# Weight transposes moved to ScalarE's queue, the second normalised copy replaced by a broadcast row, and the evacuations moved behind the state product

## The reference

```python
xn = (x - mean) / sqrt(var + 1e-5)
# recurrent branch
x2 = xn * rsqrt(mean(xn*xn) + 1e-6) * norm_w
f = maximum(sigmoid(x2 @ w_forget.T), 0.9);  v = x2 @ w_input.T;  o = sigmoid(x2 @ w_output.T)
h = f[..., None]*h + (1-f)[..., None]*v[..., None, :];  y = o * h.sum(-1)   # per head
s = xn + y
# feed-forward branch
e = argmax(xn @ W_router);  inter = gelu(xn @ W1[e] + b1[e])
g = silu(layer_norm(inter @ Wo + bo + xn))
out = x + s * g
```

## Time and profile before

| | us |
|---|---|
| median of two runs | 3336.88 |
| the profiled execution | 3346.98 |
| span of its slowest core, core 0 | 3345.2 |
| spans of all cores | 3309.5 to 3345.2 |
| TensorE busy over the span | 2899.7 (87%) |
| VectorE busy | 705.6 (21%) |
| ScalarE busy | 470.0 (14%) |

### The profile page before, as it was taken

How to read it: one execution, slowest core, us unless ns; L and a number is a source line. 1 busy time by engine, 2 the same in 40 slices (tenths; PEclk the granted TensorE clock), 3 DMA queues, 4 the chain that set the end, 5 groups by cost and what they waited for, 6 DMA issues and landing times.

```text
span 3345.2 us, 32665 instructions; the slowest of 8 cores (3309.5 to 3345.2 us)
## 1 busy us (share of the span) xinstructions
PE 2899.7 (87%) x13376; PEld 1266.5 (38%) x13376; DVE 705.6 (21%) x1289; ACT 470.0 (14%) x733; POOL 245.2 (7%) x349
## 2 busy tenths in 40 slices
PE   0247787877999999999999999999999999999994
PEld 0113333333443444443444444444444444444342
DVE  0326665751003100210111012002200310121003
ACT  1122223210000111020112011101110011102001
POOL 1014353400000000000000000000000000000000
PEclk9768998888999999999999999999999999999997
DMA  9999999945343454435344533433454345434531
GB/s 132 105 124 118 129 155 126 104 86 181 139 154 135 139 176 151 138 140 176 139 151 139 182 145 145 175 146 139 151 176 152 138 139 178 175 113 142 172 126 63
DMA packets 262385, 476.14 MB, mean 142 GB/s; under 512 B 204700, under 2 KB 204700, under 8 KB 216988
## 3 DMA queue, kind: packets, MB, share of 16 engines
q1 hardware_dynamic: 79424, 341.87, 31.4%
q0 software_dynamic: 182816, 132.18, 24.7%
HBM read 482.44 MB, written 81.79 MB: 169 GB/s over the span
## 4 chain that ended last, share of the span: by engine, by line
PE 70%; DMA 4%; DVE 1%; issue 1%; ACT 1%; DVEq 0%; SPq 0%; ACTq 0%; POOL 0%; POOLq 0%
PE pre L622 53%; PE y2a L643 7%; PE y2b L643 6%; DMA w1sl<-w1s 4%; PE pre L629 2%; DVE y L679 0%; DVE y L675 0%; PE pmu L656 0%; DMA wosl<-wos 0%; PE y2b L648 0%; PE y2a L648 0%; PE pmu L572 0%; PE psq L661 0%; DVEq L96 0%; ACT g_bf L761 0%
## 5 line engine op out<-in xcount | busy, mean ns | idle before, releaser
L622 PE MATMUL pre<-maskedA,w1sl 128*128 128x512 bf16 x8192 | 1836.0, 383 | 53.3 <-DMA w1sl<-w1s 53.3
L622 PEld LDWEIGHTS pre<-maskedA,w1sl 128*128 128x128 bf16 x8192 | 786.9, 99 | 1036.6 <-issue 143.6
L785 ACT ACTIVATE interA<-pre 128x512 bf16<-128x512 f32 x256 | 152.9, 597 | 1768.0 <-PE pre L629 1767.8
L643 PE MATMUL y2a<-interA,wosl 128*128 128x512 bf16 x1024 | 241.4, 397 | 2.3 <-DMA wosl<-wos 1.3
L643 PE MATMUL y2b<-interA,wosl 128*128 128x512 bf16 x1024 | 226.2, 379 | 0.0
L718 DVE COPY mask_bf<-pmb 4x512 bf16<-4x512 bf16 x8 | 3.3, 412 | 987.9 <-PE pmb L589 987.9
L162 POOL DMA_DIRECT2D w1s<-w x256 | 187.7, 755 | 296.4 <-issue 296.4
L456 PE MATMUL pj<-xn_fm,wfT 128*128 128x512 bf16 x512 | 121.9, 398 | 77.1 <-ACT f_fm L243 48.8
L417 PE MATMUL trA<-ident_bf,xn_tm 128*128 128x128 bf16 x256 | 34.0, 275 | 140.6 <-DVEq L96 103.6
L643 PEld LDWEIGHTS y2a<-interA,wosl 128*128 128x128 bf16 x1024 | 103.1, 101 | 138.3 <-issue 28.6
L456 PE MATMUL pj<-xn_fm,wiT 128*128 128x512 bf16 x512 | 121.2, 398 | 33.6 <-DVE v_bf L325 19.5
(11 more groups left out here) (115 smaller groups left out, 1244.6 us busy)
## 6 DMA issues: line engine op xcount, KB each, us to landing
w1sl<-w1s SPq DMA_DIRECT2D x256, 1024.0 KB, 5.3
wosl<-wos POOLq DMA_DIRECT2D x64, 1024.0 KB, 5.7
w1s<-w POOLq DMA_DIRECT2D x256, 128.0 KB, 22.3
x_a<-x SPq DMA_DIRECT2D x8, 2048.0 KB, 17.7
x_b<-x SPq DMA_DIRECT2D x8, 2048.0 KB, 17.3
out<-y POOLq DMA_DIRECT2D x8, 2048.0 KB, 8.4
wos<-wo POOLq DMA_DIRECT2D x8, 1024.0 KB, 49.5
xnbf_s<-xn_fm SPq DMA_DIRECT2D x8, 1024.0 KB, 22.8
```

The source lines that it names most:

```text
L622: ins = te.matmul(pre[b][:, :], w1sl[gi % 2][:, off:off + 128], maskedA[:, (e * KC + k) * TT:(e * KC + k + 1) * TT], start=first, stop=False)
L643: ins = te.matmul(y2[b][:, :], wosl[wi_ % 2][:, ic * 128:(ic + 1) * 128], interA[:, ic * TT:(ic + 1) * TT], start=(ic == 0), stop=False)
L785: ti(sc.activation(interA[:, i_abs * TT:(i_abs + 1) * TT], pre[b][:, :], AF.Gelu), "pre_F%d" % b, 1)
```

## The change

- **Weights.** The three casts go out in the order forget, input, output on one semaphore (`s_wnat`). The 24 transposing DMAs are issued by ScalarE (`wt_transposes`), in turn 0, behind `accums(1)` and `sqrtf(1)`, once all three casts are done. TensorE waits once, for all 24, ahead of the first projection of tile 0.
- **Second copy.** `xn2_tm`, its 4 VectorE operations and its 32 transposes per tile are gone. VectorE computes the ratio of the two roots per token (`stt[:, 72:76]`), TensorE transposes it into a row with four 128x1 transposes, ScalarE copies the row to `rrow_bf`, TensorE spreads it over 128 partitions with one matmul into `trB[1]`, and VectorE makes `xn2_fm` from `xn_fm`, the norm's weight and `trB[1]` in 8 `scalar_tensor_tensor` operations.
- **Order on VectorE.** There is no `trevacs`. The evacuations of tile t+1 stand at the head of turn t+1, so behind lines 397 and 401 of turn t. The expert choice stands ahead of the clamp instead of behind the scan.
- Some semaphores and a list of PSUM tiles that nothing used are gone.

```diff
@@ gpsimd
-                    ti(g.dma_start(out=wnat_s[1 * D:2 * D, :], in_=wiw[:, :]), "s_wn0", 16)
-                    ti(g.dma_start(out=wnat_s[0 * D:1 * D, :], in_=wf[:, :]), "s_wn1", 16)
-                    ti(g.dma_start(out=wnat_s[2 * D:3 * D, :], in_=wow[:, :]), "s_wn2", 16)
+                    for widx, src in enumerate([wf, wiw, wow]):
+                        ti(g.dma_start(out=wnat_s[widx * D:(widx + 1) * D, :], in_=src[:, :]),
+                           "s_wnat", 16)
@@ sync
-                    W(sy, "s_wn0", 16)
-                    for k in range(KC):
-                        ti(sy.dma_start_transpose(
-                            wiT[:, k * D:(k + 1) * D],
-                            wnat_s[1 * D:2 * D, k * 128:(k + 1) * 128]), "s_wt", 16)
...
@@ scalar
+                    def wt_transposes():
+                        W(sc, "s_wnat", 48)
+                        for widx in range(3):
+                            for k in range(KC):
+                                ti(sc.dma_start_transpose(
+                                    wTs[widx][:, k * D:(k + 1) * D],
+                                    wnat_s[widx * D:(widx + 1) * D, k * 128:(k + 1) * 128]),
+                                   "s_wt", 16)
...
                     for t in range(NT):
+                        W(sc, "trB_R0", t + 1)
+                        ti(sc.copy(rrow_bf[0:1, :], trB[0][0:1, 0:TT]), "s_rrow", 1)
                         if t + 1 < NT:
                             sqrtf(t + 1)
+                        if t == 0:
+                            wt_transposes()
@@ vector, xnts
-                        for sub in range(SUB):
-                            v.tensor_scalar(xn2_tm[:, sub * D:(sub + 1) * D],
-                                            x_buf[t % 2][:, sub * D:(sub + 1) * D],
-                                            stt[:, 8 + sub:9 + sub], stt[:, 44 + sub:45 + sub],
-                                            OP.subtract, OP.mult)
+                        v.reciprocal(stt[:, 68:72], stt[:, 40:44])
+                        v.drain()
+                        v.tensor_tensor(stt[:, 72:76], stt[:, 44:48], stt[:, 68:72], OP.mult)
                         DR(v, "sv_xn", "s_xfree")
@@ vector, head of turn t (trevacs is gone)
+                        for k in range(KC):
+                            g_ = 8 * t + k
+                            p_ = g_ % 2
+                            W(v, "trA_R%d" % p_, g_ // 2 + 1)
+                            ti(v.tensor_copy(xn_fm[t % 2][:, k * TT:(k + 1) * TT],
+                                             trA[p_][:, :]), "trA_F%d" % p_, 1)
+                        DR(v, "ss_xnev")
+                        W(v, "trB_R1", t + 1)
+                        for k in range(KC):
+                            v.scalar_tensor_tensor(xn2_fm[:, k * TT:(k + 1) * TT],
+                                                   xn_fm[t % 2][:, k * TT:(k + 1) * TT],
+                                                   norw_cm[:, k:k + 1], trB[1][:, :],
+                                                   OP.mult, OP.mult)
+                        DR(v, "sv_x2ev", "trB_F1")
@@ tensor
                         W(te, "sv_lgF", t)
+                        W(te, "s_rrow", t)
+                        for sub in range(SUB):
+                            ins = te.transpose(trB[0][0:1, sub * 128:(sub + 1) * 128],
+                                               stt[:, 72 + sub:73 + sub], ident_f[:, :])
+                        ti(ins, "trB_R0", 1)
...
-                            W(te, "trB_F%d" % p_, g_ // 2)
-                            for sub in range(SUB):
-                                ins = te.transpose(
-                                    trB[p_][:, sub * 128:(sub + 1) * 128],
-                                    xn2_tm[:, sub * D + k * 128: sub * D + (k + 1) * 128],
-                                    ident_bf[:, :])
-                            ti(ins, "trB_R%d" % p_, 1)
+                        W(te, "trB_F1", t)
+                        W(te, "s_rrow", t + 1)
+                        ti(te.matmul(trB[1][:, :], ones_bf[0:1, :], rrow_bf[0:1, :],
+                                     start=True, stop=True), "trB_R1", 1)
...
                         W(te, "sv_x2ev", t + 1)
+                        if t == 0:
+                            W(te, "s_wt", 16 * 24)
                         for pi, wT in enumerate([wiT, wfT, woT]):
-                            if t == 0:
-                                if pi == 0:
-                                    W(te, "s_wt", 16 * 8)
...
```

More of the change, by code:

```diff
@@ L123, in build_core @@
                    EA(nc.psum_tensor("trA1", [128, TT], BF16))]
[L124 to L125 removed]
+            trB = [EA(nc.psum_tensor("trB0", [128, TT], F32)),
+                   EA(nc.psum_tensor("trB1", [128, TT], F32))]
+            rrow_bf = EA(nc.sbuf_tensor("rrow_bf", [1, TT], BF16))
             pj = [EA(nc.psum_tensor("pj0", [128, TT], F32)),
@@ L328, in _ @@
                             xnts(t + 1)
[L329 to L332, removed]
-                            v.tensor_scalar(f_fm[:, c * TT:(c + 1) * TT],
-                                            f_fm[:, c * TT:(c + 1) * TT], FORGET_LB, None,
-                                            OP.max)
-                        v.drain()
-                        for h in range(KC):
-                            b = h % 2
-                            W(v, "vb_R%d" % b, 4 * t + h // 2 + 1)
-                            ti(v.scalar_tensor_tensor(negu_bf[:, h * TT:(h + 1) * TT],
-                                                      f_fm[:, h * TT:(h + 1) * TT], 1.0,
-                                                      vbp[b][:, :], OP.subtract, OP.mult),
-                               "vb_F%d" % b, 1)
-                        v.drain()
-                        if t % 4 != 0:
-                            nS3 = negS_bf[:, :].rearrange("p (h tt) -> p h tt", h=KC)
-                            v.tensor_copy(carry[:, :].rearrange("p (h o) -> p h o", o=1),
-                                          nS3[:, :, TT - 1:TT])
-                            v.drain()
-                        for h in range(KC):
-                            init = 0.0 if t % 4 == 0 else carry[:, h:h + 1]
-                            v.tensor_tensor_scan(negS_bf[:, h * TT:(h + 1) * TT],
-                                                 f_fm[:, h * TT:(h + 1) * TT],
-                                                 negu_bf[:, h * TT:(h + 1) * TT],
-                                                 init, OP.mult, OP.add)
-                        if t + 2 < NT:
-                            vstats(t + 2)
                         W(v, "s_lgR", t + 1)
@@ L392, in _ @@
                         v.drain()
-                        if t + 1 < NT:
-                            trevacs(t + 1)
+                        for c in range(KC):
+                            r = 24 * t + 8 + c
+                            b = r % 2
+                            W(v, "pj_F%d" % b, r // 2 + 1)
+                            v.tensor_scalar(f_fm[:, c * TT:(c + 1) * TT],
+                                            f_fm[:, c * TT:(c + 1) * TT], FORGET_LB, None,
+                                            OP.max)
+                        v.drain()
+                        for h in range(KC):
+                            b = h % 2
+                            W(v, "vb_R%d" % b, 4 * t + h // 2 + 1)
+                            ti(v.scalar_tensor_tensor(negu_bf[:, h * TT:(h + 1) * TT],
+                                                      f_fm[:, h * TT:(h + 1) * TT], 1.0,
+                                                      vbp[b][:, :], OP.subtract, OP.mult),
+                               "vb_F%d" % b, 1)
+                        v.drain()
+                        if t % 4 != 0:
+                            nS3 = negS_bf[:, :].rearrange("p (h tt) -> p h tt", h=KC)
+                            v.tensor_copy(carry[:, :].rearrange("p (h o) -> p h o", o=1),
+                                          nS3[:, :, TT - 1:TT])
+                            v.drain()
+                        for h in range(KC):
+                            init = 0.0 if t % 4 == 0 else carry[:, h:h + 1]
+                            v.tensor_tensor_scan(negS_bf[:, h * TT:(h + 1) * TT],
+                                                 f_fm[:, h * TT:(h + 1) * TT],
+                                                 negu_bf[:, h * TT:(h + 1) * TT],
+                                                 init, OP.mult, OP.add)
+                        if t + 2 < NT:
+                            vstats(t + 2)
                         W(v, "ss_o", t + 1)
```

35 lines of the change are left out of this document (8 added, 27 removed).

## The result

| | before | after |
|---|---|---|
| median of the runs, us | 3343.82 | 3386.95 |
| ratio, with its 95% interval | 1 | 1.0125 (1.0099 to 1.0151) |
| profiled execution, span of the slowest core | 3345.2 | 3386.7 |
| spans of all cores | 3309.5 to 3345.2 | 3360.8 to 3386.7 |

The changed kernel is 1.25% slower, about 42 us.

A forecast was written before the change was run, and what follows sets the result against it. Stage A's compute, not the casts, was taken as the bound. Tile 0's start at 237 us plus a 565 us chain put the last `s_bf` at 802 instead of 740.2, +62: 3337 + 62 = 3399 us, range 3358 to 3434.

The forecast's parts named there:

- the start: Stage A, tile 0: first projection waits for all 24 ScalarE-issued transposes, 110 + 24 x 4.75 + 13 = 237 us, instead of 130.42.
- What bounds: End of stage A: compute sets it; casts of stage B's weights end at 696 us, 44 us before the last `s_bf`.
- The period: Stage A, from one tile's first projection to the next: 72.6 us for six periods, where five took 70.4 before.
- the two state products: VectorE's lines 397 and 401, now on the path in each period: 4.42 + 2.29 = 6.7 us.
- the new operation with hand-over: Eight `scalar_tensor_tensor` per tile on VectorE, estimated from line 340: 5.3 us, and 0.3 until TensorE starts.
- P(0): The moment at which tile 0's first projection starts in stage A: 130.42 us before, forecast 237.
- The bound from below: Lower estimate for tile 0's first projection, at 4.1 us per transpose and 3.4 landing: 212 us.
- The sum: Last `s_bf` at 237 + 565 = 802 instead of 740.2, +62 us; stage B unchanged; 3399 us in all.
- The holes: TensorE's idle 28.3 and 36.5 us in tile 0, and 3.3 and 1.7 per period, vanish; x of tile 2 issued near 102.
- the rival with the quick transposes: Tile 0's transposes get all the engines, 24 issues shrink to about 74 us: first projection at 190, 3352 us; chance 0.12.
- Slower transposes: Rival at tile 0: new neighbours slow transposes to 5.9 us each, first projection at 264, 3426 us; chance 0.14.
- The lower clock for all of `wiT`: Rival in each period: TensorE stays slow after its pause, 7.4 us instead of 1.8, 3445 us; chance 0.06.

The follow-up runs named there:

- the kernel with the transposes on ScalarE alone: Kernel before, with ScalarE issuing the 24 transposes behind the roots of tile 1, casts on one semaphore, one TensorE wait for all: 1.0131.
- the start undone: Changed kernel with the weights' casts, SyncE-issued transposes and TensorE's three waits as before; broadcast row and late evacuations stay; run twice: 1.0005 and 0.9993.
- the late evacuations alone: Kernel before, with the paired evacuations of tile t+1 moved behind lines 397 and 401 of tile t: 0.9980.
- the kernel with the casts behind: Changed kernel, but GpSimd starts the casts of stage B's weights only when all 24 transposes have landed: 0.9877.
- three waits: Changed kernel with casts, groups and TensorE's three waits ordered as before, one ahead of each projection, transposes still issued by ScalarE: 1.0072.
- five edits that end the compute 30 to 124 us sooner: Before with early x loads, 0.9892; plus three vectors late, 0.9903; early x plus early expert choice, 0.9884; changed with stage B's casts behind transposes, 0.9877; combined, 0.9872.
- the one with 124: Kernel before with stage B's casts behind the transposes (SyncE), early x loads, three stage B vectors late, expert choice ahead of the clamp: 0.9872.

## Why the prediction came out as it did

The forecast was 3399 us and +62; it came to 3387 and +42 (+50 against the two runs that the forecast started from), on the side that was forecast and inside the range. The mechanism is the one forecast, and the start is the term that was too large.

- **What bounds.** That the casts have room in stage A was right: in a window of core 1 from 640 to 780 us the DMA engines fall idle after the eleventh slice of 3.5 us, near 678 us, and `s_bf` is done at 787.0.

```profile
DMA  9999999999400000000000436000000000000000
```

- **The period.** 72.6 was forecast; tile 3 took 514.68 - 441.70 = 73.0, and the mean over the cores is 72.1. Term by term on tile 3, forecast and measured: `wiT` 15.8 and 15.3; `wfT` 14.5 and 14.4; column sums 6.3 and 6.2; `woT` to the last sigmoid 16.1 and 17.0; statistics 3.0 and 2.9; the two state products 6.7 and 6.7; copies with hand-over 4.55 and 4.6 (504.19 to 508.8); the new operation with hand-over 5.6 and 5.6. The unseen `scalar_tensor_tensor` (estimated from line 340) took 5.36 for 8. From P(0) to the end: 565 and 561.9.
- **The start** is the term that was mis-sized. P(0) was put at 237 and came at 225.1 on core 1 (221.2 in the mean). The first issue was at 113.4, not 110; the pace was 101.2/24 = 4.2 us, not 4.75; the landing took 10.5, not 13. The mean of 4.75 had the slow first eight in it (5.9), and it is core 0's alone: over the cores of the same trace it is 4.5, which would give 232. The new neighbours (x of tile 2, `xn_fm`), for which the forecast took the long landing, didn't slow the issue: no group of eight went slower than 4.6 on this core. The same code in the kernel with the transposes on ScalarE alone took up to 5.3 on its core 1, so the pace itself varies. The bound from below was 212.
- **The sum.** Between the slowest cores the last `s_bf` moved by 787.0 - 740.2 = 46.8 us instead of 62 (12 by the start, 3 by the chain), and what follows it by 2599.7 - 2605.0 = -5.3: together 41.5.
- **The holes** went as forecast: x of tile 2 issued at 105.67, no wait for `v_bf`, 0.4 us at most for `f_fm`.
- **Two slips that the sum didn't feel.** The lower bound of 2.8 us for eight copies is not in the rows (the earlier trace rows give 8 x 0.415 = 3.3), and in the rival with the quick transposes the share of 57.8% gives 24 x 4.75 x 0.578 = 66 us and not 74.
- **Where the argument was weak though the sum was right.** The text compares a new period of 72.6 with one of 70.4, and so gives the tail a good 13 us and the start the rest. 70.4 is core 0's. The cores of the same trace reach from 69.8 to 73.1, the mean is 71.8, and a second trace has 72.6. The tail costs nothing that can be timed: 1.0005 and 0.9993 with the start undone, 0.998 with the late evacuations alone. The whole timed loss comes with the start alone (1.0131). The traces say more. From `woT` of tile 0 to the last `s_bf` it is 524 to 527 us in the five traces with the whole new tail, and 510 to 515 in the three with the old one and late x loads, so the new tail does lengthen the chain, by some 10 to 15 us. Stage B is shorter beside it, by 12 to 15 us in the two traces with the start undone, where it makes up for the chain, but only by 1 to 5 in the changed kernel. So the tail's share of the 42 us isn't settled: the timed runs leave it nothing, give or take 10, and the traces up to 14 on the chain. Why stage B is shorter is open. The total wasn't hurt, since I built the new chain to its absolute end rather than adding differences.
- **The rivals.** Slower transposes: no. The lower clock for all of `wiT`: no, 64 matmuls took 15.47 to 16.9 us, 1.5 to 2.9 over the 13.97 of the kernel with late evacuations. In the changed kernel TensorE stands 4.67 us before them, and the granted clock was 0.50, the lower level (1.2 GHz), from 514 to 519 us on core 1 and 0.96 from 519 to 531; in the kernel with late evacuations TensorE runs transposes from 397.4 up to the projection, and the clock was 1.00 from its first matmul at 404 on (core 7). Quick transposes: the mechanism is real, but needs the casts out of the way, which the change doesn't do; I had named that as the reason against. The Trainium skill (DMA: Bandwidth & Descriptors, Latency and other measured facts) gives 261 GB/s for transposing DMAs, measured on one kernel. Core 0 of the kernel with the casts behind moved 6.15 MB in a window of 47 us, 131 GB/s, and the changed kernel 5.89 MB in 110 us, 54 GB/s; neither reaches the page's rate.
- **The issuing engine.** A transpose took 4.3 us of issuing from ScalarE (102.6/24 in the mean of the cores) and 4.5 from SyncE (108.7/24). The Trainium skill (DMA: Bandwidth & Descriptors, Issuing engines are not separate DMA queues) says that DMAs run on the same 16 DMA engines whichever engine issued them; the traces agree, since the pace hardly changed with the issuer.

## What to carry to other kernels

When weights are prepared beside the first tile, the order in which their parts land and what else queues behind their issue decide the start; one wait for the last of them throws away all overlap, and an engine that issues them can't do its own work meanwhile (with three waits, ScalarE's first sigmoid came at 228 us, right behind its last issue). Before giving a difference of a few us per period to a cause, look at the period on all cores and in a second trace: here it spread by more than the effect. And look for the next bound before adding gains up: five edits that end the compute 30 to 124 us sooner were all worth 32 to 43 us in time. For the one with 124 the trace shows why, since the transfers beside it set the end from about 690 us on; for the others the differences lie within the intervals.

## What the runs showed of the hardware

- Transposing and casting DMAs that run together slow each other down. 24 transposes of 256 KB: 102.6 us of issuing beside the casts, 43.6 without (means of the cores). On core 0 the casts were issued from 5.8 to 654.7 us with the transposes among them, 649 us, and from 142.5 to 695.7 behind them, 553 us: 96 us less for the same casts (92 in the mean of the cores, 635 and 543). The longer stretch also shares the engines with the three weight casts and the first x loads, so the 96 is an upper bound for what the mixing costs the casts.
- Starting the transposes 50 us earlier, beside x loads and casts, moved their last issue by 11 us only.
- After a pause of about 21 us that ends with 4.67 us of idleness, TensorE ran the next 64 matmuls in 15.47 us at a granted clock of 0.66 (442 to 446 us, tile 3 on core 1) and then 1.00; after a pause that ended in 7 us of transposes it ran them in 13.97, at 1.00 throughout (core 7, late evacuations).
- Issuing 8 transposes held ScalarE's queue for 30.6 to 42.5 us beside the casts, and for 13.2 to 17.4 us without them (the rows above). In the kernel with three waits ScalarE's next work, the first sigmoid, started behind the last issue.
